# Cross-attention loop: the four scores of a chunk issued together, ahead of both parts of the projections

## What is computed

```python
Q = _proj(query, Wq, bq)          # 256 rows, 16 heads of 32
K = _proj(key, Wk, bk)            # 25088 rows (the context)
V = _proj(value, Wv, bv)          # 25088 rows (the context)
scores = jnp.einsum('bihd,bjhd->bijh', Q, K) * SCALE
attn = jax.nn.softmax(scores, axis=1)                      # over the 256 queries
x = jnp.einsum('bijh,bjhd->bihd', attn, V).reshape(B, S, D_MODEL)
return x @ Wo + bo
```

## Time and profile before

| | |
|---|---|
| time, 3 runs | 2586.2 us median (2585.86 to 2586.34) |
| span of the profiled execution | 2583.4 us (the page gives no other time of it) |
| busy share of the span | PE 99%, DVE 75%, ACT 71%, POOL 48% |
| TensorE instructions of the stage | L725 x3136, L695 x2352, L713 x1584, L734 x6272 |
| first and last weight load of L725 | 496 us and beyond 2125 us |

### The profile page before, as it was taken

The page is one execution under the profiler, slowest core; times in us unless marked ns, Lnnn a source line. Parts: engine busy times, 40 slices in busy tenths (PEclk is TensorE's granted clock), DMA queues, the critical chain, the costliest instruction groups (busy, mean ns, idle before and its releaser), DMA issues.

```text
span 2583.4 us, 54302 instructions
## 1 busy us (share of the span) xinstructions
PE 2551.2 (99%) x18734; PEld 2070.9 (80%) x18734; DVE 1938.3 (75%) x3664; ACT 1826.9 (71%) x6852; POOL 1245.5 (48%) x2033
## 2 busy tenths in 40 slices
PE   8999999999999999999999999999999999999998
PEld 6877999877777777777777777777777775899997
DVE  8876866688778788888887787888888875665555
ACT  2215444388888888888888888888888886455453
POOL 5433111365655555655556555556555543222222
PEclk9999999999999999999999999999999999999999
DMA  9996443667766677676677666676766663545451
GB/s 391 387 357 225 184 184 147 176 164 175 166 165 163 163 172 171 163 175 159 164 176 165 165 161 167 170 172 163 173 160 165 159 134 135 193 186 196 180 184 69
DMA packets 132420, 472.98 MB, mean 183 GB/s; under 512 B 31144, under 2 KB 31272, under 8 KB 124848
## 3 DMA queue, kind: packets, MB, share of 16 engines
q1 hardware_dynamic: 124896, 456.14, 62.8%
q10 hardware_dynamic: 7248, 13.37, 1.4%
HBM read 244.47 MB, written 17.30 MB: 101 GB/s over the span
## 4 chain that ended last, share of the span: by engine, by line
PE 95%; DVE 2%; ACT 1%; DMA 1%; issue 0%; POOL 0%; SPq 0%; DVEq 0%; POOLq 0%
PE PB L695 21%; PE PB L725 15%; PE PB L734 14%; PE PB L713 14%; PE PB L820 7%; PE PB L835 7%; PE PB L655 6%; PE PB L501 5%; PE PB L668 3%; ACT EE L1004 1%; PE PB L544 1%; DMA AR<-in_ctx 1%; PE PB L601 1%; PE PB L551 1%; DMA W<-in_l0x 0%
## 5 line engine op out<-in xcount | busy, mean ns | idle before, releaser
L1004 ACT ACTIVATE EE<-PB,small 128x256 f32<-128x256 f32 x3136 | 1435.7, 497 | 207.2 <-DVE small L1376 199.2
L1376 DVE TENSOR_REDUCE small<-PB 128x2 f32<-128x512 f32 x1568 | 1029.4, 684 | 316.1 <-PE PB L725 312.4
L1004 ACT ACTIVATION_READ_ACCUMULATOR EE<-PB,small 128x1 f32 x3136 | 719.7, 230 | 0.0
L725 PEld LDWEIGHTS PB<-QS,STK 128*128 128x128 f32 x3136 | 558.1, 188 | 177.6 <-issue 41.0
L695 PE MATMUL PB<-CTX,WKV 128*128 128x512 f32 x2352 | 680.6, 394 | 0.0
L1644 POOL TENSOR_TENSOR VS<-V,small 128x128 f32<-128x128 f32 x784 | 331.5, 423 | 678.3 <-DVE small L1382 678.1
L725 PE MATMUL PB<-QS,STK 128*128 128x256 f32 x3136 | 617.1, 286 | 7.5 <-ACT EE L1004 7.1
L713 PE MATMUL PB<-WKV,CTX 128*128 128x512 f32 x1584 | 469.2, 393 | 0.0
L695 PEld LDWEIGHTS PB<-CTX,WKV 128*128 128x128 f32 x2352 | 385.1, 189 | 29.4
L734 PE MATMUL PB<-EE,VS 128*32 128x256 f32 x6272 | 368.9, 383 | 0.0
L734 PEld LDWEIGHTS PB<-EE,VS 128*32 128x32 f32 x6272 | 191.5, 110 | 131.7 <-issue 3.1
(11 more groups left out here) (216 smaller groups left out, 2504.4 us busy)
## 6 DMA issues: line engine op xcount, KB each, us to landing
STK<-KHL SPq DMA_DIRECT2D x1568, 128.0 KB, 2.4
RW<-in_l1f SPq DMA_DIRECT2D x32, 2048.0 KB, 7.9
AR<-in_ctx SPq DMA_DIRECT2D x49, 1024.0 KB, 8.3
RAW<-in_ctx SPq DMA_DIRECT2D x98, 512.0 KB, 3.9
WF<-in_l0f SPq DMA_DIRECT2D x17, 2304.0 KB, 9.0
V<-v_scr SPq DMA_DIRECT2D x64, 256.0 KB, 3.0
v_scr<-RAW ACTq DMA_DIRECT2D x49, 256.0 KB, 7.4
RW<-in_l1a SPq DMA_DIRECT2D x1, 4096.0 KB, 13.7
```

The lines of the kernel that those rows point to most:

```text
L725: m = e.matmul(bank(2 * (k % 2) + half, 256 * (s % 2), 256), STK[:, g % 2, s, c % 2, j:j + 128], QS[:, s, c, :], start=True, stop=True)
L1004: m = e.activation(EE[:, b, s, :], bank(2 * (k % 2) + half, 256 * (s % 2), 256), ACT.Exp, bias=nm[:, b, s:s + 1], accum_out=su[:, b, s:s + 1])
L1376: e.tensor_reduce(nm[:, k % RING, 2 * half:2 * half + 2], bank(2 * (k % 2) + half).rearrange("p (s i) -> p s i", s=2), axis=AX.X, op=ALU.m ...
```

## The change

Inside the loop over chunks the special cases for the first and the last chunk of six go away. In every chunk both halves of the scores come first, then both steps of projections, then (at k%6 = 5) the mixes. No instruction is added or removed; programs of the other engines are not touched.

```diff
             for k in range(NCH):
-                first, last = k % MIX == 0, k % MIX == MIX - 1
                 scores(k, 0)
-                if first:
-                    scores(k, 1)
+                scores(k, 1)
                 project(k, 0)
-                if last:
-                    project(k, 1)
-                if not first:
-                    scores(k, 1)
-                if not last:
-                    project(k, 1)
+                project(k, 1)
                 if k % MIX == MIX - 1:
                     for n in range(max(k - MIX - 1, 0), k - 1):
                         mix(n)
```

## The result

| | before | after |
|---|---|---|
| time, 5 runs each | 2586.2 us (2584.79 to 2586.34) | 2650.02 us (2649.8 to 2651.5) |
| span of the profiled execution | 2583.4 us | 2649.5 us |

The changed kernel takes 1.0252 times as long, with a 95% interval of 1.024 to 1.0263: 64 us between the medians, 66.1 us between the two profiled spans.

What follows compares the result with a forecast made beforehand. TensorE was taken to bound the loop. Waits of 0.57 + 0.44 = 1.01 us per twelve chunks, times 65, add 66 us to the 2583.4 us span; with 2.8 us to the median and 1 us off, 2651 us, range 2624 to 2674.

Steps and rivals of the forecast that it cites:

- Scores in fours cost nothing: On TensorE, four scores in a row cost what two pairs cost; 0.01 us either way each, -6 to +6 us.
- The gate opens 0.05 us behind the exponentials, and the 16th of them does not move: Scores load 0.05 us after ScalarE's read; a half's 16th exponential stays 8.91 us behind its opening scores.
- +0.57 and +0.44 us per half: Mixes start later by this much in chunks 0 to 5 and 6 to 11, since the last scores wait for exponentials.
- The rule: Loss per half: projections moved behind the gate (0.93 or 1.39), less slack above 0.05 (0.24 or 0.83), less 0.12 of cover.
- Waits inside a half are part of the last one: Waits of 0.41 us in chunk 3 and some 0.1 in chunk 10 add nothing beyond the 0.57 and 0.44.
- The cover that a load loses: A scores' weight load no longer hidden under a running projection on TensorE; 0.12 us, subtracted in the loss per half.
- The step from projections to mixes: TensorE's change of matmul shape ahead of the mixes, at 130 places: taken as 0.09 us, 0 to 0.20 possible.
- Closed gaps: Gaps in ScalarE's run close, gates come 0.25 and 0.15 us sooner: 40 us loss, 2626 us; chance 0.10.
- feedback: Held-up K projections delay VectorE's moves, maxima, ScalarE and the next gate: 20 us more, 2671 us; chance 0.12.
- No change: TensorE does not stand still for a gate because later work goes first: 2586 us; chance 0.03.
- Faster: Projections ahead of the mixes hide the step between shapes (12 us), with gates open: 2574 us; chance 0.03.
- The clock: TensorE's clock falls to half speed for a tenth of the loop: 166 us more, 2817 us; chance 0.02.

Runs made afterwards that it cites:

- experiment 5: Changed kernel with exponentials over 128 of the 256 queries from chunk 8 on: 2583.68 us, ratio 0.9994 to the kernel before.
- experiment 6: Kernel before with exponentials over 128 of the 256 queries from chunk 8 on, order of scores unchanged: 2578.76 us, ratio 0.9975.
- experiment 4: Kernel before with the new order only in chunks k%12 = 1, 2, 7, 8 and 9: 2586.98 us, ratio 1.0004.
- the last gate alone: Kernel before with the new order in the last chunk of six only: 2651.19 us, ratio 1.0252.
- the inner ones alone: Kernel before with the new order in all but the last chunk of six: 2621.36 us, ratio 1.0138.
- experiment 3: Kernel before with only the special case of the last chunk of six removed, so it alternates like the middle ones: 2595.69 us, ratio 1.0038.
- Experiment 8: Kernel before with mixes every 7 chunks instead of 6 and the scores of a block's last two chunks put later: 2592.71 us, ratio 1.0028.

## Why the prediction was right, point by point

**TensorE bounds the loop and has no slack.** Right: in experiment 5 a faster ScalarE took back what the order had cost, all but the 4.9 us by which it stays behind experiment 6, and in experiment 6 it gave a quarter of a per cent. The 3 us to which I had bounded that case missed the end of the loop.

**Scores in fours cost nothing.** Right within the bound that was given, 0.01 us each: 0.47 us in the chain, 2587.0 against 2585.7 us in experiment 4, inside the interval. The traces show 0.04 us more per stretch there, for five fours.

**The gate opens 0.05 us behind the exponentials, and the 16th of them does not move.** Right on both counts, 0.05 and 8.91 us; in the second half the 16th ends 8.73 us behind the opening scores before (1329.08 - 1320.35) and 8.76 after (1335.66 - 1326.90). It was the step on which the sum hung, and it was safe for the reason given: ScalarE's run starts from scores that the change leaves in place, and its gap hangs on a `k_raw` that does not move. In the chain after, that `k_raw` is the very piece that leads to S(3,1).

**+0.57 and +0.44 us per half.** Right: 13.05 us from mixes to mixes in the first half and 13.36 in the second half shown, where 13.05 and 13.33 were forecast. Over the halves of the loop the medians are 12.47 and 12.91 us before and 13.04 and 13.33 after, so +0.57 and +0.42. At chunk 756 the scores behind the mixes start at these times, before and after:

```profile
2093.74 0.74 PE L725 MATMUL PB<-QS,STK 128*128 128x256 f32 x4
```

```profile
2157.07 0.62 PE L725 MATMUL PB<-QS,STK 128*128 128x256 f32 x3
```

63.3 us later after 63 stretches, 1.005 us each against 1.01 forecast. The spans differ by 66.1, so the last 28 chunks add 2.8 us. The rule gives 2.0 for the two stretches left there, I had taken 1 us off for the first stretch and the last chunks, and it is some 1 us more. These chunks have fewer projections, and TensorE stands at the gates in both kernels (for the kernel before, see the waits in experiment 6).

**From the span to the median.** Here two small errors went opposite ways, which is luck. The span was put at 2583.4 + 65 = 2648 and is 2649.5; the median of the runs was put 2.8 us above it and is 0.5 above (2650.02 and 2649.5). The time of the profiled execution after is 1.7 us above its own span (2651.22 and 2649.5). With the same 1.7 before, the other 1.1 of the 2.8 came from a profiled execution that was a little faster than the median.

**Waits inside a half are part of the last one.** Right, and the best tested point: 2651 with the last gate alone, 2621 with the inner ones alone, where 2651 and 2621 were on record.

**The cover that a load loses.** Right in kind and size: 0.11 us in the chain of experiment 3, where the rule gave 0.10.

**Projections at 0.232 us each.** Right: five take 1.16 to 1.17 us in the chains of experiment 5 and of the changed kernel too. The figure of the Trainium skill (TensorE: Matmul & The Clock Gate, Back-to-back issue gap), 131 ns, gave an estimate of 10 us for the loss; the runs side with the row.

**The step from projections to mixes.** Taken as 0.09 with 0 to 0.20 open. The mixes start where 0.09 puts them, 10.32 us into the first half, so the bounds of -12 to +14 us were not needed.

**What would show it.** One sign was wrong. I had written that the waits of the scores for exponentials would grow from 3.0 to some 60 us. From 820 to 2130 us the view of waits shows for the changed kernel:

```profile
ACT EE L997 <- DVE small L1369: 194.5, 99, 2.2
PEld PB L725 <- ACT EE L997: 39.9, 130, 0.4
```

There are 39.9 us on loads and no line for the matmuls. By the legend of the page the end of a matmul is modelled; a wait of 0.4 us is, it seems, mostly covered by the modelled end of the matmul ahead of it. The sign that did hold is ScalarE's idle time before its exponentials, by the page 199.2 us before and 264.0 after: 64.8 us more, the loss itself.

**The rivals.** Closed gaps (2626) and feedback (2671) did not come: the exponentials' times against the opening scores are the same in both kernels. No change needed TensorE to let later work past a shut gate; the load of S(3,1) stands still for 0.35 us instead (1345.57 above), and the projections behind it come after it. Faster needed gates that open sooner, which only experiment 5 made. The clock did not fall in the loop's stretches: the granted clock of the changed kernel is 1.00 from 496 to 2190 us. It falls only at the end of the loop, as before: 0.58 from 2203 to 2211 us, against 0.51 from 2136 to 2143.

## What to carry to other kernels

This is what one kernel shows, so take it as a way of reading and not as a law. On an engine that works its list in order, an instruction with a gate belongs behind the independent work and not ahead of it, even if the engine is 99% busy: what counts is how late the gate opens against the place in the list. The cost of moving it ahead can be worked out from two numbers, the independent work that it jumps over and the slack that it had (and, for some tenth of a microsecond here, the work that no longer covers its load), and here it was the last gate before the engine's next long block that set the sum, because the gates counted from ScalarE's own run and not from TensorE's waits. Experiment 8 is the warning: put later, the scores still met waits, and others came in. Look for that slack at the end of the pattern, where the fast engine has caught up with the slow one, and not in an average over the loop.

## What the runs showed of the hardware that I had not expected

A wait of up to half a microsecond on TensorE hardly shows as idle time: the changed kernel's TensorE is drawn busy for 2605.8 us instead of 2551.2 with the same 18734 matmuls. Across weight loads, matmuls and idle time the loss shows in full only in the chain and in the idle time of ScalarE, the engine that TensorE waits for.

The step from full-array matmuls (128x128) to the mixes (128x32) is the same 0.09 us behind a pair of scores of 256 columns, before, and behind projections of 512 columns, after: there the load starts at 1349.22, the mixes start at 1350.58, and of the 1.36 us between them 0.34 are the load and two scores and 0.93 the four projections.
